# Two-layer attention and mixture of experts on one core: the block list spread over partitions, slots and products moved

## Chip, core and metric

The kernel runs on one core of one Trainium2 chip. The metric is the device time of one execution in microseconds (us), here given as the median of several runs. Engines are named as in the profile: PE (TensorE, with PEld for its weight loads), DVE (VectorE, "Vector"), ACT (ScalarE), POOL (GpSimd) and SP (SyncE, which here only issues DMAs).

## What is computed

The reference, cut to what matters: x has 32 sequences of 128 tokens of 128 features, the context 32 times 77 tokens.

```python
x = x + L0_xattn(layernorm(x), ctx, ctx)    # 16 heads of 8, softmax over 77 keys
x = x + L0_moe(layernorm(x))                # 8 experts, top 2, silu(x W1) * (x W2) @ W3, F = 256
x = x + L1_xattn(layernorm(x), ctx)         # softmax over features: q + q (k^T v) / (q sum k)
x = x + L1_moe(layernorm(x))                # 2 shared experts + 8 experts, top 2, gelu, F = 512
# top 2: topv, topi = top_k(xt @ Wg.T, 2); w = softmax(topv); out = sum over the 2 of w * expert(xt)
```

## The kernel before

Activations of all 32 tiles of 128 tokens stay in on-chip memory (`x_sb`). Work goes by 8 groups of 4 tiles (`NGRP`, `U_LAST` is group 7). Each layer is an attention part (`attention0`, `attention1`) that also routes its tokens, and a part `routed(l)` in which 40 blocks of tokens go through the experts.

Routing. For each group Vector chooses two experts per token (`choose`), PE counts them (`column_sums`, then `ranks`), GpSimd computes the exponent of the difference of the two logits (`gate_exp`), Vector makes the gates (`gates`) and the row to which each token goes (`slots`), and GpSimd scatters the rows of the group, 8 indirect DMAs, into a DRAM buffer sorted by expert (`scatter(l, group, from, to)`). After the last group's ranks PE sums the counts of all experts (semaphore `counts`, its matmul writes the same row of counts into 128 partitions). From it Vector makes the ends of the regions (`region_tails`, which lets SyncE and ScalarE write padding rows there, five and three DMAs) and the list of blocks (`block_list`, semaphore `emap`): for each of 32 slots for big blocks (256 rows) and 32 for small ones (128 rows) the expert, the first row, and a count that the load of the rows waits for. The last group's `slots` must be done before its rows are scattered; when all rows have landed GpSimd writes `mark` (semaphore `sorted`). Every Vector instruction in `block_list` waits for the one before by a semaphore (`link`).

Routed blocks. SyncE loads, in the order written in its program, the weights of 5 blocks ahead (`block_weights`) and the rows of 6 blocks ahead (`block_rows`); both read the block's numbers from the list `e_i` into registers. First blocks of the list may be spare; only rows of real ones wait for `sorted`. PE takes the blocks in order: transposes, up products, down products. Vector and ScalarE do the rest, and GpSimd scatters the results back to token order. PE enters `routed(0)` when `emap`, `bias1_ready` and `cx_v` for all groups are there. `bias1_ready` is Vector's last instruction in `attention0`, behind all of its `context_shift`s.

Context of layer 1. In layer 0's end the keys and values of the context are made for layer 1: PE does `context_keys(g)` and `context_values(g)`, Vector subtracts the maximum (`context_shift(g)`, two instructions), ScalarE copies values (`context_values`) and takes exponents (`context_exp`). `context_keys(g)` has two banks in turn and waits for the shift of group g - 2. `keep_clock(n, b)` issues n products of constants on 512 columns into bank b that nobody reads.

Order at the end of `attention0` on Vector, before: inverse sums of group 7, gates and slots of group 5, output and residual of group 7, choice of group 6, `context_shift(0)`, gates and slots of group 6, `context_shift(1)`, choice of group 7, `context_shift(2)`, tails, the list, `context_shift(3)`, gates and slots of group 7, the other shifts. In layer 1 gates and slots of group 7 stand before the list already.

Of the kernel before, what the change touches and what calls it, by code (L numbers as in the profile page):

```python
# [25 lines left out]
I32 = mybir.dt.int32  # L26
# [4 lines left out]
P = 128  # L31
# [6 lines left out]
E = 8  # L38
# [53 lines left out]
K_SPARE = K_INDEX + 2 * NSLOT  # L92
K_DONE = K_SPARE + 2 * NSLOT
# [6 lines left out]
def constants():  # L100
# [14 lines left out]
    i = np.arange(NSLOT)  # L115
    c[:, K_INDEX:K_SPARE] = np.concatenate([BLK * (i - NBIG), P * (i - NSMALL)])
    spare = E * PITCH + DSMALL * P
    c[:, K_SPARE:K_DONE] = np.repeat([spare + DBIG * BLK, spare], NSLOT)
# [102 lines left out]
def build(nc, a, out):  # L221
    ctx = ExitStack()
    with ctx:
# [59 lines left out]
        cnt = sb("cnt", [1, E])  # L283
        cnt_i = sb("cnt_i", [1, E], I32)
        til_i = sb("til_i", [1, 2, E], I32)
        til = sb("til", [1, 2, E])
        upto = sb("upto", [1, 2, E, E])
        cum = sb("cum", [1, 2, E])
        excess = sb("excess", [1, 1])
        split = sb("split", [1, E])  # L290
        edge = sb("edge", [1, 2, E + 1])
        whole = sb("whole", [1, E])
        base = sb("base", [1, 2, E])
# [5 lines left out]
        inside = sb("inside", [1, 2, NSLOT, E])  # L299
        index = sb("index", [1, 2, NSLOT])  # L300
        spare = sb("spare", [1, 2, NSLOT])
        e_i = sb("e_i", [1, 3, 2 * NSLOT], I32)
        erow = sb("erow", [1, 3, 2 * NSLOT])
# [4 lines left out]
        until = sb("until", [1, len(SETS)])  # L308
        below = sb("below", [1, len(SETS), NYB * NQ])
# [84 lines left out]
        def _(sp):  # L394
# [41 lines left out]
            def routed(l):  # L436
# [4 lines left out]
                def block_weights(u):  # L441
                    after(sp, S("y_sum"), u - NWB + 1)
                    b = column_of(u)
                    e = sp.value_load(e_i[0:1, 0, b:b + 1], min_val=0, max_val=E - 1)
                    sp.dma_start(w_blk[u % NWB][:, 0:wc], wsrc[bass.ds(e, 1)].rearrange("o p c -> p (o c)"))\
                        .then_inc(S(f"w_in{u % NWB}"), 16)

                def block_rows(u):
                    after(sp, S(f"y_out{u % NYB}"), stored(u - NXR + NYB))
                    b, n = column_of(u), tiles_of(u)  # L450
                    r = sp.value_load(e_i[0:1, 1, b:b + 1], min_val=0, max_val=E * PITCH + SPARE - n * P)
                    if u < first_real:
                        count = sp.value_load(e_i[0:1, 2, b:b + 1], min_val=1, max_val=3)
                        sp.wait_ge(S("sorted"), count)
# [53 lines left out]
        def _(pool):  # L508
# [47 lines left out]
            def attention0():  # L556
# [317 lines left out]
        def _(dve):  # L874
# [71 lines left out]
            def block_list(l):  # L946

                link(v.tensor_scalar(cnt[:], bank[4 - l][0:1, 0:E], float(P - 1), None, ALU.add))
# [4 lines left out]
                link(v.scalar_tensor_tensor(til[:, 1, :], til[:, 0, :], -2.0, til[:, 1, :], ALU.mult, ALU.add))  # L953
                link(v.tensor_tensor(upto[:], til[:].unsqueeze(2).to_broadcast([1, 2, E, E]),
                                     cst[0:1, K_LE:K_INDEX].rearrange("p (k a b) -> p k a b", k=2, a=E), ALU.mult))
# [3 lines left out]
                link(v.tensor_tensor(split[:], cum[:, 0, :], excess[:].to_broadcast([1, E]), ALU.min))  # L959
                link(v.tensor_tensor(edge[:, 0, 1:E + 1], cum[:, 0, :], split[:], ALU.subtract))  # L960
                link(v.tensor_tensor(edge[:, 1, 1:E + 1], cum[:, 1, :], split[:], ALU.add))

                def over_slots(ap):
                    return ap.unsqueeze(2).to_broadcast([1, 2, NSLOT, E])

                link(v.tensor_tensor(index[:], cst[0:1, K_INDEX:K_SPARE].rearrange("p (k i) -> p k i", k=2),
                                     edge[:, :, E:E + 1].to_broadcast([1, 2, NSLOT]), ALU.add))
# [3 lines left out]
                link(v.tensor_scalar(erow[:, 0, :], erow[:, 0, :], -1.0, 0.0, ALU.add, ALU.max))  # L971
                link(v.tensor_scalar(erow[:, 2, :].rearrange("p (k i) -> p k i", k=2), inside[:, :, :, 0], float(l + 1), 1.0,
                                     ALU.mult, ALU.add))

                link(v.tensor_tensor(whole[:], edge[:, 0, 1:E + 1], edge[:, 0, 0:E], ALU.subtract))
                link(v.tensor_tensor(base[:], cst[0:1, K_BASE:K_N].unsqueeze(1).to_broadcast([1, 2, E]), edge[:, :, 0:E],
                                     ALU.subtract))
                link(v.tensor_tensor(base[:, 1, :], base[:, 1, :], whole[:], ALU.add))
                link(v.tensor_tensor(inside[:], inside[:], over_slots(base[:]), ALU.mult))
                link(v.reduce_max(spare[:], inside[:], AX.X))  # L980
                row = erow[:, 1, :].rearrange("p (k i) -> p k i", k=2)
# [865 lines left out]
```

## Time and profile before

| | us |
|---|---|
| median of 3 runs | 782.66 (781.25 to 784.82) |
| the profiled execution | 784.91 |
| its span, first to last instruction | 782.9 |
| PE busy in it | 688.5 |
| Vector busy in it | 465.7 |
| GpSimd busy in it | 381.2 |
| ScalarE busy in it | 327.3 |

The mean granted clock of PE is 0.942 of full speed. The chain of work that ended last is 53% PE, 18% Vector, 8% issue, 5% DMA and 4% each GpSimd, ScalarE and SyncE. A busy share is a mean over the whole span; what an edit does is read where it stands. In a timeline row a bracket gives the time that the engine sat idle before, and what ended it; rows of like instructions next to each other are merged with a count.

### The profile page before, as it was taken

The numbers are of one execution on the slowest core, as the hardware profiler recorded it, in microseconds if no ns is written. First come the engines' busy times: TensorE is split into PE (matmuls) and PEld (weight loads), VectorE is DVE, ScalarE is ACT, GpSimd is POOL, SyncE is SP. The second block draws the span as 40 slices with busy tenths as digits, with TensorE's granted clock in tenths as the row PEclk, the third lists the DMA queues.
The fourth block names the chain that finished last, engine by engine and source line by source line (L and its number), as shares of the span: only waits on it lengthen the run. The fifth ranks groups of instructions, "written<-read, shape, count | busy, mean of one in ns | idle before, by whom it ended". The sixth has DMA issues, their size and how long they took to land.

```text
span 782.9 us, 15683 instructions
## 1 busy us (share of the span) xinstructions
PE 688.5 (88%) x5118; PEld 510.3 (65%) x5118; DVE 465.7 (59%) x1347; ACT 327.3 (42%) x689; POOL 381.2 (49%) x502
## 2 busy tenths in 40 slices
PE   4999999999898968889878799999999689999990
PEld 2666666566666657878766545555554389999990
DVE  2566877787677667676656667676653523324326
ACT  2344455445333232222212456667764244444440
POOL 5213176566537524555551365555555414454452
PEclk9999999999889789999997899999999979999996
DMA  6811111221101457776756000000000478877769
GB/s 164 258 12 10 10 28 26 30 30 25 32 12 35 126 166 237 215 225 204 212 165 173 0 18 21 28 29 21 24 28 27 123 234 258 270 238 246 227 196 285
DMA packets 102120, 91.34 MB, mean 117 GB/s; under 512 B 52953, under 2 KB 85849, under 8 KB 101721
## 3 DMA queue, kind: packets, MB, share of 16 engines
q1 hardware_dynamic: 86375, 68.80, 32.4%
q0 software_dynamic: 8640, 17.84, 6.4%
q10 hardware_dynamic: 7025, 3.70, 1.9%
q8 instruction: 42, 0.69, 0.4%
q14 instruction: 38, 0.30, 0.1%
HBM read 69.13 MB, written 22.72 MB: 117 GB/s over the span
## 4 chain that ended last, share of the span: by engine, by line
PE 53%; DVE 18%; issue 8%; DMA 5%; POOL 4%; ACT 4%; SPq 4%; another core or an unknown queue 3%; POOLq 0%; DVEq 0%; ACTq 0%
PE pair L1352 27%; PE pair L1640 10%; PE pair L1355 8%; DVE sm L1116 3%; DVE smax L1112 3%; POOL xs_sorted L553 2%; DMA xr<-xs_sorted 2%; PE pair L1458 2%; PE pair L1692 2%; PE pair L1473 2%; ACT xa L663 2%; DMA y_tok<-ysb,xr 1%; DMA xa<-y_tok 1%; DVE bns L1062 1%
## 5 line engine op out<-in xcount | busy, mean ns | idle before, releaser
L626 POOL DMA_INDIRECT y_tok<-ysb,xr x142 | 137.6, 969 | 145.5 <-DVE ysb L1032 116.3
L553 POOL DMA_INDIRECT xs_sorted<-xa,slot_i x128 | 130.2, 1017 | 93.5 <-DVE slot_i L939 59.0
L1352 PE MATMUL pair<-xT,w_all 128*128 128x256 f32 (+1 forms) x640 | 142.9, 369 | 0.0
L1640 PE MATMUL pair<-w_all,hT 128*128 128x128 f32 x852 | 110.8, 279 | 10.1 <-DVE hT L1019 10.0
L1352 PEld LDWEIGHTS pair<-xT,w_all 128*128 128x128 f32 x640 | 112.6, 201 | 10.4
L1640 PEld LDWEIGHTS pair<-w_all,hT 128*128 128x128 f32 x852 | 108.1, 195 | 15.1 <-issue 12.0
L801 ACT ACTIVATE hT<-pair,w_all 128x256 f32<-128x256 f32 (+1 forms) x160 | 62.0, 448 | 78.6 <-PE pair L1352 78.1
L1011 DVE COPY xT<-pair 128x256 f32<-128x256 f32 (+1 forms) x80 | 31.5, 394 | 104.9 <-PE pair L1355 88.7
L797 ACT ACTIVATE hg<-pair,w_all 128x256 f32<-128x256 f32 (+1 forms) x80 | 31.7, 447 | 93.5 <-PE pair L1352 68.3
L1112 DVE TENSOR_REDUCE smax<-pair 128x8 f32<-128x616 f32 x64 | 50.5, 788 | 33.2 <-PE pair L1352 32.8
L1352 PE MATMUL pair<-xeT_all,w_sh 128*128 128x512 f32 x128 | 69.2, 623 | 0.0
L818 ACT ACTIVATE hS<-pair,w_sh 128x512 f32<-128x512 f32 x64 | 43.9, 686 | 53.5 <-PE pair L1352 43.2
L1692 PE MATMUL pair<-hS,w_sh 128*128 128x512 f32 x128 | 65.4, 593 | 0.0
L1355 PEld LDWEIGHTS pair<-cst,sm 128*128 128x128 f32 x320 | 37.2, 151 | 26.4 <-issue 26.4
L1355 PE MATMUL pair<-cst,sm 128*128 128x128 f32 x320 | 52.8, 300 | 0.2 <-issue 0.2
L1116 DVE TENSOR_TENSOR sm<-pair,smax 128x616 f32<-128x616 f32 x64 | 51.2, 799 | 2.2
L1352 PE MATMUL pair<-hT,yS 32*128 32x308 f32 x192 | 41.8, 514 | 11.6 <-DVE sm L1116 10.0
L1355 PE MATMUL pair<-cst,xr 128*128 128x128 f32 x142 | 30.7, 288 | 18.7 <-DMA xr<-xs_sorted 7.0
L1019 DVE SCALAR_TENSOR_TENSOR hT<-pair,w_all,hg 128x256 f32<-128x256 f32 (+1 forms) x80 | 32.6, 448 | 24.2 <-remote 15.1
L701 ACT ACTIVATE wide<-pair 128x384 f32<-128x384 f32 x64 | 24.5, 434 | 44.5 <-PE pair L1355 44.5
L701 ACT ACTIVATE hS<-pair 128x384 f32<-128x384 f32 x64 | 24.6, 433 | 34.3 <-PE pair L1355 34.3
L1692 PEld LDWEIGHTS pair<-hS,w_sh 128*128 128x128 f32 x128 | 23.0, 190 | 23.7 <-issue 21.2
(194 smaller groups left out, 1100.5 us busy)
## 6 DMA issues: line engine op xcount, KB each, us to landing
w_all<-in_w SPq DMA_DIRECT2D x40, 578.0 KB
w_all<-in_w SPq DMA_DIRECT2D x40, 450.0 KB
xa<-y_tok SPq DMA_DIRECT2D x32, 256.0 KB, 5.6
xr<-xs_sorted SPq DMA_DIRECT2D x62, 130.0 KB
y_tok<-ysb,xr POOLq DMA_INDIRECT x142
xs_sorted<-xa,slot_i POOLq DMA_INDIRECT x128
out<-x_sb ACTq DMA_DIRECT2D x8, 256.0 KB, 3.1
xs_sorted<-in_pads SPq DMA_DIRECT2D x12, 130.0 KB, 4.3
```

The source lines that it names most:

```text
L553: g.indirect_dma_start(xs_dram[l], bass.IndirectOffsetOnAxis(ap=slot_i[:, i:i + 1], axis=0), xa[:, GT * c + j // TOPK, j % TOPK, :], None) ...
L626: g.indirect_dma_start(y_dram[l], bass.IndirectOffsetOnAxis(ap=xr[u % NXR][:, t, P:P + 1].bitcast(I32), axis=0), ysb[u % NYB][:, t, :], None)\
L701: s_.activation(pT[T % 2][gr][:, 0:n], bank[2 + gr % 2][:, 0:n], ACT.Exp, scale=SCALE)\
L801: s_.activation(hT[k][:, c, 0:n], src, ACT.Gelu, bias=w[:, bcol + c:bcol + c + 1])\
L818: s_.activation(hS[i % 4][:], bank[4 + i % 2][:], ACT.Gelu, bias=w_sh[:, col:col + 1])\
L1019: v.scalar_tensor_tensor(hT[k][:, c, 0:n], chunk(bank[2 * k + 1], c, BLK)[:, 0:n], w[:, bcol + c:bcol + c + 1], hg[k][:, c, 0:n], ALU.add, ...
L1112: link(v.reduce_max(smax[ab][:].rearrange("q (b h) -> q b h", b=2), score(ab), AX.X))
L1116: v.tensor_tensor(sm[ab][:, 0:SPAN].rearrange("q (b h k) -> q b h k", b=2, k=NK), score(ab), smax[ab][:].rearrange("q (b h) -> q b h", b=2 ...
L1352: return mm(out_, l_, r_, start=True, stop=True)
L1355: return nc.tensor.transpose(out_, in_, ident)
L1640: last = mm(bank[4 + k][:, t * P:(t + 1) * P], hT[k][:, c, t * P:(t + 1) * P], chunk(w, nu + c, P), start=(c == 0), stop=(c == nc_ - 1))
L1692: mm(bank[6][:], w_sh[:, wd:wd + P], hS[i % 4][:], start=(c == 0), stop=(c == NC1S - 1))\
```

## The change

`block_list` is computed with one slot per partition: partitions 0 to 31 hold the big slots, 32 to 63 the small ones. Each partition computes the counts for itself (on 64 partitions in place of one), and `inside`, which had 2 x 32 x 8 elements in one partition, has 8 in each of 64. The results `e_i` are 64 x 3 in place of 1 x 192, so the registers are loaded from another partition for each slot. The number of linked instructions goes from 26 to 27, and `low_counts`, inside `routed`, gets one more. The table of constants is 95 columns narrower. Vector's order changes: gates and slots of group 5 go in front of the inverse sums of group 7; gates and slots of group 7 go in front of the tails and the list, and `context_shift(2)` and `(3)` behind it. GpSimd's scatters of group 5 are split once more around `gate_exp` of group 6. PE gets four products of constants in three places.

```diff
@@ constants
-K_SPARE = K_INDEX + 2 * NSLOT
-K_DONE = K_SPARE + 2 * NSLOT
+K_AT = K_INDEX + NBIG
+K_SPARE = K_AT + 1
+K_DONE = K_SPARE + 1
@@ SyncE
-                    e = sp.value_load(e_i[0:1, 0, b:b + 1], min_val=0, max_val=E - 1)
+                    e = sp.value_load(e_i[b:b + 1, 0:1], min_val=0, max_val=E - 1)
...
@@ GpSimd, attention0
                 inverse_std(0, 1, "lne", U_LAST)
+                scatter(0, U_LAST - 2, 4, 6)
                 gate_exp(0, U_LAST - 1)
-                scatter(0, U_LAST - 2, 4, NPS)
+                scatter(0, U_LAST - 2, 6, NPS)
@@ Vector, block_list
-                link(v.tensor_scalar(cnt[:], bank[4 - l][0:1, 0:E], float(P - 1), None, ALU.add))
+                both, big, small = slice(0, 2 * NSLOT), slice(0, NSLOT), slice(NSLOT, 2 * NSLOT)
+                link(v.tensor_scalar(cnt[:], bank[4 - l][both, 0:E], float(P - 1), None, ALU.add))
...
-                link(v.tensor_tensor(inside[:], over_slots(edge[:, :, 0:E]),
-                                     index[:].unsqueeze(3).to_broadcast([1, 2, NSLOT, E]), ALU.is_le))
-                link(v.reduce_sum(erow[:, 0, :].rearrange("p (k i) -> p k i", k=2), inside[:], AX.X))
+                link(v.tensor_tensor(edge[big, 1:E + 1], cum[big, 0, :], split[big, :], ALU.subtract))
+                link(v.tensor_tensor(edge[small, 1:E + 1], cum[small, 1, :], split[small, :], ALU.add))
+
+                link(v.tensor_tensor(base[big, :], cst[big, K_BASE:K_N], edge[big, 0:E], ALU.subtract))
+                link(v.tensor_tensor(base[small, :], cst[small, K_BASE:K_N], edge[small, 1:E + 1], ALU.subtract))
+                link(v.scalar_tensor_tensor(base[small, :], til[small, 1, :], float(P), base[small, :], ALU.mult, ALU.add))
+
+                link(v.tensor_tensor(index[:], cst[both, K_AT:K_SPARE], edge[:, E:E + 1], ALU.add))
+                link(v.tensor_tensor(inside[:], edge[:, 0:E], index[:].to_broadcast([2 * NSLOT, E]), ALU.is_le))
+                link(v.reduce_sum(erow[:, 0:1], inside[:], AX.X))
...
+                link(v.tensor_tensor(inside[:], inside[:], base[:], ALU.mult))
+                link(v.reduce_max(begin[:], inside[:], AX.X))
...
@@ Vector, attention0
-                inverse_sums(U_LAST)
                 gates(0, U_LAST - 2)
                 slots(0, U_LAST - 2)
+                inverse_sums(U_LAST)
...
                 sums(0, U_LAST)
-                context_shift(2)
+                gates(0, U_LAST)
+                slots(0, U_LAST)
                 region_tails(0)
                 block_list(0)
-                context_shift(3)
-                gates(0, U_LAST)
-                slots(0, U_LAST)
-                for g in range(4, NGRP):
+                for g in range(2, NGRP):
                     context_shift(g)
@@ PE, attention0
                 context_values(1)
+                keep_clock(1, 4)
                 column_sums(0, U_LAST - 1)
                 ranks(0, U_LAST - 1)
+                keep_clock(2, 4)
                 kept_turned(U_LAST)
                 context_values(2)
                 logits(U_LAST)
                 context_keys(2)
                 context_values(3)
+                keep_clock(1, 4)
                 pe.wait_ge(S("slots"), U_LAST)
                 column_sums(0, U_LAST)
```

## Rows read from the trace of the kernel before

**Rows 1.** The page, its first line.
```profile
span 782.9 us, 15683 instructions
```
**Rows 2.** The chain that ended last, in order: start us, us, what.
```profile
269.12 4.01 another core or an unknown queue
...
279.28 0.46 PE pair L1355
```
**Rows 3.** Timeline of all engines, 266 to 290: start us, us, engine, line, operation.
```profile
268.42 1.08 PE L1389 MATMUL pair<-bias,ones_row 1*77 1x512 f32 x2
...
270.36 1.04 PE L1352 MATMUL pair<-wa,xeT_all 128*77 128x128 f32 x8
...
277.46 0.59 ACT L660 ACTIVATE kvm_all<-pair 77x512 f32<-77x512 f32 x1 [7.53 <-remote]
```
**Rows 4.** Timeline of GpSimd (POOL), layer 0, then layer 1.
```profile
266.06 0.96 POOL L553 DMA_INDIRECT xs_sorted<-xa,slot_i  x1 [4.56 <-DVE slot_i L939]
...
274.92 0.96 POOL L553 DMA_INDIRECT xs_sorted<-xa,slot_i  x1 [0.30 <-issue]
...
618.71 0.96 POOL L553 DMA_INDIRECT xs_sorted<-xa,slot_i  x1 [0.30 <-issue]
```
**Rows 5.** Timeline of SyncE's DMA issues (SP), layer 0, then layer 1.
```profile
256.39 8.66 SPq L462 DMA_DIRECT2D xs_sorted<-in_pads  x5
...
273.09 0.00 SPq L445 DMA_DIRECT2D w_all<-in_w  x1
...
277.44 0.33 SPq L445 DMA_DIRECT2D w_all<-in_w  x1
...
281.82 1.97 SPq L457 DMA_DIRECT2D xr<-xs_sorted  x2
...
287.90 0.33 SPq L457 DMA_DIRECT2D xr<-xs_sorted  x1
...
608.38 5.75 SPq L462 DMA_DIRECT2D xs_sorted<-in_pads  x5
...
622.76 0.34 SPq L445 DMA_DIRECT2D w_all<-in_w  x1
...
625.52 0.33 SPq L445 DMA_DIRECT2D w_all<-in_w  x1
```
**Rows 6.** Timeline of Vector (DVE), layer 1, last instruction of the list.
```profile
616.47 0.25 DVE L986 CAST e_i<-erow 1x192 int32<-1x192 f32 x1
```
**Rows 7.** Timeline of Vector, layer 0, the list of blocks.
```profile
255.21 0.15 DVE L948 TENSOR_SCALAR cnt<-pair 1x8 f32<-1x8 f32 x1
...
257.97 0.75 DVE L968 TENSOR_TENSOR inside<-edge,index 1x512 f32<-1x512 f32 x1
258.76 0.67 DVE L970 TENSOR_REDUCE erow<-inside 1x64 f32<-1x512 f32 x1
...
262.75 0.25 DVE L986 CAST e_i<-erow 1x192 int32<-1x192 f32 x1
```
**Rows 8.** Timeline of all engines: Vector at the inverse sums.
```profile
232.47 0.96 DVE L1125 RECIPROCAL rden<-pair 128x128 f32<-128x128 f32 x1 [1.50 <-PE pair L1473]
```
**Rows 9.** Timeline of Vector, first instruction of the last group's gates.
```profile
264.24 0.16 DVE L921 TENSOR_SCALAR wsum<-exd 128x4 f32<-128x4 f32 x1
```
**Rows 10.** Stretches: length, busy time by engine, granted clock, DMA share, GB/s.
```profile
245.00:250.00 5.00, 4.70 (x22) 4.03 (x22) 3.27 (x14) 1.95 (x4) 3.78 (x5) 0.66 0.15 45
...
260.00:265.00 5.00, 5.00 (x17) 3.41 (x18) 4.59 (x15) 1.37 (x3) 1.20 (x2) 0.50 0.30 74
...
275.00:280.00 5.00, 0.45 (x1) 0.18 (x1) 1.81 (x4) 2.52 (x5) 0.96 (x2) 0.59 0.47 143
```
**Rows 11.** Timeline of PE in layer 0 around the choices.
```profile
243.25 0.19 PE L1352 MATMUL pair<-ones_b,oh 128*64 128x1 bf16 x1 [0.60 <-DVE high L906]
...
245.30 1.11 PE L1355 MATMUL pair<-cst,xa 128*128 128x128 f32 x4 [0.97 <-ACT xa L663]
```
**Rows 12.** The chain that ended last, in layer 1.
```profile
603.81 0.86 PE pair L1692 x2
```

More of the change, by code:

```diff
@@ L282, in build @@
         csum = sb("csum", [P, NCH, P], BF16)
[L283 to L293, printed above, removed]
+        cnt = sb("cnt", [2 * NSLOT, E])
+        cnt_i = sb("cnt_i", [2 * NSLOT, E], I32)
+        til_i = sb("til_i", [2 * NSLOT, 2, E], I32)
+        til = sb("til", [2 * NSLOT, 2, E])
+        units = sb("units", [2 * NSLOT, 2, E])
+        upto = sb("upto", [2 * NSLOT, 2, E, E])
+        cum = sb("cum", [2 * NSLOT, 2, E])
+        excess = sb("excess", [2 * NSLOT, 1])
+        split = sb("split", [2 * NSLOT, E])
+        edge = sb("edge", [2 * NSLOT, E + 1])
+        base = sb("base", [2 * NSLOT, E])
         tail_i = sb("tail_i", [1, E], I32)
@@ L298, in build @@
         slot_i = sb("slot_i", [P, NPAIR], I32)
[L299 to L303, printed above, removed]
+        inside = sb("inside", [2 * NSLOT, E])
+        index = sb("index", [2 * NSLOT, 1])
+        begin = sb("begin", [2 * NSLOT, 1])
+        e_i = sb("e_i", [2 * NSLOT, 3], I32)
+        erow = sb("erow", [2 * NSLOT, 3])
         mark = sb("mark", [1, 1])
@@ L308, in build @@
         until = sb("until", [1, len(SETS)])
+        last = sb("last", [1, 1])
         below = sb("below", [1, len(SETS), NYB * NQ])
@@ L978, in block_list @@
[L978 to L981, printed above, removed]
-                link(v.scalar_tensor_tensor(row, index[:], 0.0, cst[0:1, K_SPARE:K_DONE].rearrange("p (k i) -> p k i", k=2),
-                                            ALU.is_lt, ALU.mult))
@@ new lines, in block_list @@
+                link(v.tensor_scalar(erow[:, 0:1], erow[:, 0:1], -1.0, 0.0, ALU.add, ALU.max))
+                link(v.tensor_scalar(erow[:, 2:3], inside[:, 0:1], float(l + 1), 1.0, ALU.mult, ALU.add))
+                link(v.tensor_tensor(inside[:], inside[:], base[:], ALU.mult))
+                link(v.reduce_max(begin[:], inside[:], AX.X))
+                link(v.tensor_tensor(begin[:], begin[:], index[:], ALU.add))
+                link(v.scalar_tensor_tensor(erow[:, 1:2], index[:], 0.0, cst[both, K_SPARE:K_DONE], ALU.is_lt, ALU.mult))
@@ L986, in block_list @@
+                link(v.tensor_tensor(erow[:, 1:2], erow[:, 1:2], begin[:], ALU.add))
                 v.tensor_copy(e_i[:], erow[:]).then_inc(S("emap"), 1)
@@ L990, in low_counts @@
                 n = len(SETS)
-                link(v.tensor_tensor(until[:], pre[:], edge[:, 0, E - 1:E].to_broadcast([1, n]), ALU.add))
-                link(v.tensor_tensor(below[:, :, NSTILL:NB], index[:, 0, ISTILL:NBIG].unsqueeze(1)
+                link(v.tensor_tensor(last[:], edge[0:1, E - 1:E], edge[0:1, E:E + 1], ALU.subtract))
+                link(v.tensor_tensor(until[:], pre[:], last[:].to_broadcast([1, n]), ALU.add))
+                link(v.tensor_tensor(below[:, :, NSTILL:NB], cst[0:1, K_INDEX + ISTILL:K_AT].unsqueeze(1)
                                      .to_broadcast([1, n, NB - NSTILL]),
```

34 lines of the change are left out of this document (11 added, 23 removed).

## Prediction

> **What bounds it now.** I read the page for the span, 782.9 us [rows 1], then the chain that ended last through the two places where the list of blocks is made, then each engine's timeline there. The reader is to see three things. First, in layer 0 the routed blocks start on PE at 279.28, behind the bias addition on Vector, and the chain in front of it holds 4.01 us put down to "another core or an unknown queue" [rows 2]. PE began its last values product of the context at 270.36, yet ScalarE copied those values at 277.46, after 7.53 us of idling [rows 3]: PE's signals arrived late. Second, this lateness coincides with GpSimd's scatters issued back to back. The last group's eight run from 266.06 to 275.88, and the lateness ends 1.6 us after; ahead of them stands a pause of 4.56 [rows 4]. SyncE is slow in the same stretch: its weight loads at 273.09 and 277.44 stand 4.35 apart, where 2.75 is normal without scatters (622.76 to 625.52) [rows 5]. Third, in layer 1 nothing but SyncE's order of loads stands before the blocks: the list is written at 616.72, the second weights leave at 622.76 [rows 5, 6], and PE follows the rows loaded between them.
>
> **The list of blocks.** Before, 26 linked Vector instructions from 255.21 to 263.00, 7.8 us [rows 7]; in layer 1 the same ones end at 616.72 [rows 6]. After, 27. Those on 8 elements stand 0.19 apart. Four work on 512 elements in one partition, 0.75 and 0.67, and then the same pair again [rows 7]; they become 8 elements in 64 partitions. I price them as 0.15 and a gap of 0.04: 4 x 0.19 = 0.76 in place of 3.0, so 2.25 less. Seven on 64 or 192 elements (0.25 for the last [rows 7]) shrink by 0.3 together. One instruction more costs 0.19. Sum: 2.35 less, 5.4 us. No row shows few elements in exactly 64 partitions; the row with 128 partitions and 4 elements (0.16 [rows 9]) and those with 512 bound the list between 5.4 and, were none of the four to shrink, 7.9. I take 5.4, by the nearest row. The Trainium skill, "VectorE: DVE Perf Modes", section on SBUF-source operations' fixed extra latency, gives the time as a constant plus the elements of the free dimension; by its 58 cycles at 0.96 GHz an instruction on 8 elements would take some 0.07, an estimate that the rows' 0.16 replaces.
>
> **Layer 1.** Its order is untouched, so the list ends at 616.72 - 2.35 = 614.4. SyncE ends its five tail loads at 614.13 (608.38 plus 5.75 [rows 5]) and waits for the list, so the loads of block 0 leave 2.2 us earlier. From 616.72 to the second weights at 622.76 SyncE took 6.0 where a normal pair and the way to the first load need 3.5: it is slow until about 1.5 us past GpSimd's last scatter (618.71 plus 0.96 [rows 4]). That end does not move; the loads in front of it do. Bounds: the slow stretch takes half of the gain back, -1.0, or a pair slips wholly in front of it, -2.6. I take -2.3. All later row loads follow in SyncE's order and PE follows them; behind it PE is the chain, so nothing absorbs it.
>
> **Layer 0, what is ready when.** Gates and slots of the last group begin at 264.24 [rows 9] and release GpSimd for 266.06 [rows 4]; without their way to it they take 1.55. They now stand in front of the list, from about 254.2. The tails, just before 255.21, move to about 256.2, the list ends at about 261.7 instead of 263.0. SyncE's tail loads start 0.9 later, and SyncE was busy with them until 265.05 (256.39 plus 8.66 for five [rows 5]), past the old end of the list; so the earlier list alone brings nothing. GpSimd's last eight scatters come without the pause: they end at 261.8 + 8 x 1.265 = 271.9 instead of 275.88. The mark that rows are sorted goes from about 277.5 to 273.5, but the first load that needs it left at 281.82 [rows 5]: nothing by itself.
>
> **What this collides with.** Fourteen scatters now run without a pause from about 254.3, so SyncE is slow through its tail loads (9.6 us instead of 8.66) and its first loads: weights at 267.5 and 271.8, then 2.75 a pair, rows of block 6 at 286.8 against 287.90 [rows 5]. These need block 0's result as well, some 8.6 us behind PE's start (279.28 to 287.90). So PE's start decides, unless SyncE keeps 4.3 a pair for longer. Bounds of this cap: 284 and 290.5.
>
> **Context keys behind the list.** Shifts 2 to 7 all come after it now. A keys product waits for the shift two before it, so products 4 to 7 start only at about 263.1; before, PE ran them beside the list. At full clock one costs 1.94 (268.42 to 270.36) and a values product 1.0 [rows 3]. After 263.1: four keys and three values, 10.8, a last shift 1.4, bias 0.3: blocks start at 275.6, a gain of 3.7. But PE now idles from about 258 to 263.1. In this trace the idle stretch before 279.28 took the granted clock to 0.59 in its window [rows 10], which is the 1.2 GHz level for most of it; at that level, 0.50 in 260 to 265 [rows 10], each of these products takes nearly twice as long. Some 6 to 10 us at half clock cost 3 to 5: start at 279 to 280.9. I take 279.6, +0.3. The Trainium skill, "TensorE: Matmul & The Clock Gate", section "What's actually happening", says that throttled is the default state and activity releases it. By that rule the shifts behind the list work against the change, and the trace agrees in sign.
>
> **Products in waits.** A product on 512 columns is two records, 0.86 us [rows 12]. One stands in a wait of 0.60 before 243.25, two in 0.97 before 245.30 [rows 11], the last ahead of the last group's column sums, in a wait that I take as short as the first. They overrun by 0.26, 0.75 and about 0.3. Against that, the stretch from 245 to 250 ran at 0.66 [rows 10]: with the transposes at 245.30, whose four took 1.11 [rows 11], about 1.3 comes back if the clock stays up (a third of 5 us is lost, less what waits hide). Net 0.1 late at the last group's choice; bounds -1.0 and +1.4.
>
> **Slots of the third last group in front of the inverse sums.** They fill Vector's idle 1.50 before 232.47 [rows 8] and take 1.8: inverse sums start 0.3 later. GpSimd's split of the scatters frees the norm 0.7 earlier; ScalarE has two copies of PE's values ahead of its use, so this is hidden. Cost +0.2, bounds -0.4 and +0.4. One more small instruction per layer in the counts of low rows lies in Vector's idle time beside the blocks; map entries read from other partitions are as many register loads on SyncE as before; the smaller table of constants comes in behind other inputs: nothing for each, 0.2 a load at worst for the second, hidden but for the first pairs.
>
> **Sum.** Layer 1 -2.3; start of layer 0's blocks +0.3, which has the products' 0.1 and the inverse sums' 0.2 in it, as they precede the list: -2.0. The profiled execution lasted 784.91, 2.0 more than its span, and gives 782.9; the median of the runs shown, 782.66, is 2.25 lower and gives 780.6.
>
> **Rivals.** (a) The lateness ends with the scatters, and PE keeps the full clock or regains it at once: layer 0's blocks start at 275.6, so -3.7 - 2.3, 776.7. For it: the scatters end 4 us earlier, and the late signals held 277.46. Against: PE's idling before 263.1 and SyncE's cap. Chance 0.27. (b) The other side: PE's signals are held through the run of fourteen, up to the 6.0 us of the values product at 270.36. Keys 4 reach Vector at 272.8, the shift ends at 274.2, and two keys and one values product at half clock, 9.7, a shift and the bias remain: 285.6, +6.3; with layer 1, 786.7. It decides from a start at 285.5 on. For it: the run is nearly twice as long. Against: in the run of eight Vector got the keys before the last inside it. Chance 0.1. (c) The shorter list has no effect, because the slow stretch of SyncE takes all of layer 1's gain: 782.9. Chance 0.13. My forecast, 780.6 with its own range of 778.8 to 783.5, has 0.5.
>
> **Numbers.** 0.5% is 3.9 us, about what a measurement of this kernel can tell from no change: below 778.7 is faster, above 786.6 slower. Faster takes (a) nearly whole and a little of the forecast: 0.29. Slower takes half of (b) and as much for the bounds above: 0.09. Same: 0.62. The range, 776.2 to 785.0, leaves out the tails of (a) and most of (b).
>
> **What would show it.** The list at 5.4 us in both layers; layer 1's first weights 2.2 us sooner after the tails; fourteen scatters with gaps of 0.3 alone; PE idle for 4 to 5 us before keys 4 and a granted clock near 0.5 behind it; blocks starting right behind Vector's bias. It is wrong if the list does not shrink, if the clock stays at 1.00 through the keys, or if SyncE's tails take over 12 us.

## The result, and the profile after

The changed kernel took 788.75 us (median of 7 runs, 786.04 to 790.52), the kernel before on the same chip 781.91 (7 runs, 779.52 to 785.9). The medians differ by 6.8 us. The ratio is given as 1.0081, 95% interval 1.0052 to 1.0109, which is slower by 6.3 us. The forecast was 780.6, range 776.2 to 785.0, so the time lies outside it. What came in layer 0 is rival (b), to which the forecast gave 0.1, and in layer 1 rival (c). The profiled execution of the changed kernel took 789.36 us.

The profile after is read in the order of the forecast: the span, the list, then layer 0 engine by engine, then layer 1. The page's first line:

```profile
span 787.2 us, 15704 instructions
```

The list of blocks in the changed kernel, timeline of Vector in layer 0, first two instructions, the compare and the reduction that worked on 512 elements before, and the last:

```profile
254.17 0.15 DVE L953 TENSOR_SCALAR cnt<-pair 64x8 f32<-64x8 f32 x1
254.35 0.37 DVE L954 CAST cnt_i<-cnt 64x8 int32<-64x8 f32 x1
...
257.89 0.16 DVE L974 TENSOR_TENSOR inside<-edge,index 64x8 f32<-64x8 f32 x1
258.08 0.15 DVE L975 TENSOR_REDUCE erow<-inside 64x1 f32<-64x8 f32 x1
...
259.57 0.20 DVE L983 CAST e_i<-erow 64x3 int32<-64x3 f32 x1
```

From 254.17 to 259.77 are 5.6 us, against 7.8 before [rows 7]. The two wide instructions went from 0.75 and 0.67 to 0.16 and 0.15. The list did what it was priced at.

The chain that ended last, in the changed kernel, behind the list:

```profile
262.57 0.04 issue
262.63 10.39 another core or an unknown queue
273.04 0.70 DVE cxm L1075
...
283.94 1.75 issue
285.69 0.46 PE pair L1351
```

In front of layer 0's blocks stood 4.01 us of an unnamed release before [rows 2]; now it is 10.39. The blocks start at 285.69 instead of 279.28, 6.4 later, as much as the kernel lost. The other engines say what it is made of. Timeline of GpSimd, first and last of fourteen scatters, all 0.30 apart:

```profile
252.45 1.03 POOL L556 DMA_INDIRECT xs_sorted<-xa,slot_i  x1 [0.20 <-issue]
...
268.96 0.96 POOL L556 DMA_INDIRECT xs_sorted<-xa,slot_i  x1 [0.30 <-issue]
```

Timeline of SyncE's issues in the same kernel, layer 0, then layer 1:

```profile
255.28 18.31 SPq L465 DMA_DIRECT2D xs_sorted<-in_pads  x5
274.43 0.38 SPq L448 DMA_DIRECT2D w_all<-in_w  x1
...
613.56 5.98 SPq L465 DMA_DIRECT2D xs_sorted<-in_pads  x5
623.37 0.77 SPq L448 DMA_DIRECT2D w_all<-in_w  x1
626.83 0.36 SPq L460 DMA_DIRECT2D xr<-xs_sorted  x1
627.97 0.34 SPq L448 DMA_DIRECT2D w_all<-in_w  x1
```

The five padding copies took 18.31 us to issue, where they took 8.66 before [rows 5]. SyncE came out of them 3.7 us after the last scatter's end at 269.92. Taken one by one they left at 255.28, 257.33, 262.36, 269.46 and 273.06: the gaps grow to 7.1 as the run goes on. In layer 1 the first four left 1.3 apart (613.56 to 617.49) although GpSimd's last eight scatters had begun at 614.59, so the loads are not slow beside every scatter.

Timelines of PE and then of Vector (the same kernel): the keys of shifts 4, 6 and 7 on PE, and the waits of Vector for them:

```profile
261.11 1.99 PE L1385 MATMUL pair<-bias,ones_row 1*77 1x512 f32 x2 [4.02 <-issue]
263.03 1.99 PE L1389 MATMUL pair<-wa,xeT_all 128*77 128x128 f32 x8
...
274.50 1.98 PE L1385 MATMUL pair<-bias,ones_row 1*77 1x512 f32 x2 [4.53 <-DVE hS L1076]
...
281.96 1.99 PE L1389 MATMUL pair<-wa,xeT_all 128*77 128x128 f32 x8
```
```profile
273.04 0.69 DVE L1075 TENSOR_REDUCE cxm<-pair 77x64 f32<-77x512 f32 x1 [10.47 <-remote]
...
278.44 0.69 DVE L1075 TENSOR_REDUCE cxm<-pair 77x64 f32<-77x512 f32 x1 [2.48 <-PE pair L1389]
...
283.98 0.69 DVE L1075 TENSOR_REDUCE cxm<-pair 77x64 f32<-77x512 f32 x1 [4.13 <-PE pair L1389]
```

PE had the keys of shift 4 done at 265.0, but Vector started on them only at 273.04, 3.1 us after the last scatter's end. ScalarE waited in the same way for the next values, which PE had done at 266.7 (its timeline):

```profile
273.14 0.59 ACT L664 ACTIVATE kvm_all<-pair 77x512 f32<-77x512 f32 x1 [11.42 <-remote]
```

This is called holding below. Whether PE's signal left late or the waiting engines took it late isn't told apart by these rows. Once the holding was over PE ran keys 6, values 7 and keys 7 from 274.50 to 283.95, at 1.98 and 1.99 for what takes 1.08 at full clock [rows 3]. The stretches of the changed kernel show the two clock levels (granted clock is the third number from the end):

```profile
245.00:250.00 5.00, 5.00 (x37) 3.97 (x36) 4.45 (x19) 1.71 (x3) 3.70 (x4) 1.00 0.15 45
...
270.00:275.00 5.00, 0.49 (x1) 0.33 (x2) 1.82 (x3) 1.86 (x4) 0.00 (x0) 0.92 0.08 27
275.00:280.00 5.00, 5.00 (x18) 3.32 (x16) 2.30 (x4) 0.25 (x1) 0.09 (x1) 0.50 0.66 195
280.00:285.00 5.00, 3.94 (x11) 1.94 (x10) 0.98 (x2) 1.63 (x3) 0.00 (x0) 0.50 0.58 159
```

In 245 to 250 the constants' products kept 1.00 where before had 0.66 [rows 10]. After the idle stretch up to 274.50 PE had the lower level, 0.50, for the products that decide.

In layer 1 the gain did not come. From the start of the tail loads to the second weights are 14.41 us (613.56 to 627.97), and were 14.38 (608.38 to 622.76, [rows 5]). The list was no longer what SyncE waited for: Vector wrote it by 619.9, GpSimd's last scatter ended at 624.53, and SyncE's first load of rows left 2.3 us after that. Vector's and GpSimd's timelines:

```profile
619.71 0.16 DVE L983 CAST e_i<-erow 64x3 int32<-64x3 f32 x1
```
```profile
623.57 0.96 POOL L556 DMA_INDIRECT xs_sorted<-xa,slot_i  x1 [0.30 <-issue]
```

Only the first weights left sooner, by 0.8 (9.81 after the start of the tail loads for 10.58); the first rows (13.27 for 13.25) and the second weights did not. Ten further traces of kernels with the new list on chips of this kind have 14.70 to 14.78 to the second weights, so the missing gain is no accident of one trace; before has one trace on this kind.

So the profile gives +6.4 at layer 0's blocks and nothing at layer 1's first loads. The tail loads of layer 1 stand 5.2 later than before and the span is 4.3 longer; no edit is behind what came back in between. Two traces of the changed kernel on chips of one kind differ by 8.6 us in span (787.2 and 795.8), so one trace's span isn't split finer than that here. The start of the tail loads moves too, from 252.82 to 258.26 in five traces of kernels that are alike up to there. The time from the tail loads to the blocks is steadier: 30.41 and 30.48 in two traces of the changed kernel, 22.89 in the one of before, so 7.5 longer.

### The profile page after: what moved, and what is told of

It reads as the page before. It is cut to its first block, busy times and chain, and to the rows that moved or that the text cites. A ratio compares the mean times of both kernels' runs of the same rounds, so it can differ in the third digit from the quotient of the medians.

```text
span 787.2 us, 15704 instructions
## 1 busy us (share of the span) xinstructions
PE 689.2 (88%) x5126; PEld 507.5 (64%) x5126; DVE 460.7 (59%) x1351; ACT 326.9 (42%) x689; POOL 381.9 (49%) x502
## 4 chain that ended last, share of the span: by engine, by line
PE 49%; DVE 20%; issue 10%; POOL 5%; SPq 5%; ACT 4%; DMA 3%; another core or an unknown queue 3%; POOLq 0%; DVEq 0%; ACTq 0%
PE pair L1348 26%; PE pair L1639 9%; PE pair L1351 7%; DVE sm L1114 3%; POOL xs_sorted L556 3%; DVE smax L1110 3%; PE pair L1454 2%; PE pair L1691 2%; ACT xa L667 2%; PE pair L1469 1%; DMA xr<-xs_sorted 1%; DVE bns L1060 1%; POOL rstd L536 1%; SPq L454 1%
## 5 line engine op out<-in xcount | busy, mean ns | idle before, releaser
L1348 PE MATMUL pair<-xT,w_all 128*128 128x256 f32 (+1 forms) x640 | 141.1, 365 | 0.0
L1348 PEld LDWEIGHTS pair<-xT,w_all 128*128 128x128 f32 x640 | 110.7, 198 | 10.0
L1639 PE MATMUL pair<-w_all,hT 128*128 128x128 f32 x852 | 109.0, 276 | 5.7 <-DVE hT L1017 4.3
```

The costliest lines, as they stand in the source:

```text
L1348: return mm(out_, l_, r_, start=True, stop=True)
L1639: last = mm(bank[4 + k][:, t * P:(t + 1) * P], hT[k][:, c, t * P:(t + 1) * P], chunk(w, nu + c, P), start=(c == 0), stop=(c == nc_ - 1))
```

## Experiments

Eighteen runs of twelve kernels were made, on five chips. The chips are of two kinds. On three (here the first kind) the kernel before takes 782 to 789 us, as in the first comparison; on two (the second kind) 752. All times of an experiment are compared with before on its own chip. Two theories of the loss stand behind them. T1 (A1 in the first expectations): the run of fourteen scatters holds PE's signals and SyncE's loads. T2 (A2 there): shifts 2 to 7 stand behind the list, so PE idles and then runs the keys late and at half clock. In the first expectation A is that the moves in layer 0 did the harm and not the list, B that the list or its registers cost something.

**What part of the change costs it.** The first four ran on one chip of the second kind, where before took 752.02. The new list alone, all orders and PE's program as before:

```
-                gates(0, U_LAST)
-                slots(0, U_LAST)
+                context_shift(2)
                 region_tails(0)
                 block_list(0)
-                for g in range(2, NGRP):
+                context_shift(3)
+                gates(0, U_LAST)
+                slots(0, U_LAST)
+                for g in range(4, NGRP):
                     context_shift(g)
...
-                keep_clock(1, 4)
```

> The kernel before with the new list of blocks and its narrower constants alone; every order as before. Theory A (the moves in layer 0 did the harm, the list itself helps): SyncE's five tail loads again near 9 us, blocks of layer 0 start where they did, within 1 us, layer 1's rows 2 us earlier, so 2.0 to 2.5 us below the kernel before. Rival B (the list on 64 partitions, or its registers read from many partitions, costs something in the blocks): no gain or a loss of 1 to 4 us, spread over both routed parts.

Measured: 748.27, ratio 0.9944 (0.9921 to 0.9967). The new list by itself gains 3.7 us there, more than the 2.0 to 2.5 expected. Its blocks do not start where they did: they start 15.65 us after the tail loads (245.11 to 260.76), against 20.87 for before on the other chip of this kind (245.86 to 266.73).

The last group's gates and slots behind the list again, shifts 2 to 7 behind them:

```
-                gates(0, U_LAST)
-                slots(0, U_LAST)
                 region_tails(0)
                 block_list(0)
+                gates(0, U_LAST)
+                slots(0, U_LAST)
```

> The changed kernel with the last group's gates and slots behind the list again, so that GpSimd pauses in front of its last eight scatters; shifts 2 to 7 stay behind the list. Theory A1 (fourteen scatters without a pause hold SyncE and PE's signals): tail loads back from 18.3 to about 9 us, Vector's 10.5 us wait for PE gone, blocks of layer 0 start at 280 to 281.5 on the old time axis, so 3 to 5 us below the changed kernel. Rival A2 (the harm is the shifts behind the list, which leave PE idle and at half clock): the start stays within 1.5 us of the changed kernel's 285.7.

Measured: 753.68, ratio 1.0017 (0.9990 to 1.0044). On this chip the edit did not part the run. GpSimd had only just reached the last group's scatters when their slots were written (its timeline, first of the last eight):

```profile
253.26 0.96 POOL L556 DMA_INDIRECT xs_sorted<-xa,slot_i  x1 [0.30 <-DVE slot_i L943]
```

One shift back in front:

```
+                context_shift(2)
                 gates(0, U_LAST)
                 slots(0, U_LAST)
                 region_tails(0)
                 block_list(0)
-                for g in range(2, NGRP):
+                for g in range(3, NGRP):
```

> The changed kernel with context_shift(2) in front of the gates and slots of the last group; shifts 3 to 7 stay behind the list, the run of fourteen scatters stays. Theory A1: tail loads stay near 18 us and the gain is small, 0 to 2 us below the changed kernel, as keys 4 are made during the list but their signal is held. Rival A2: PE is busy beside the list, keeps the clock, and 4 to 5 us come back.

Measured: 748.85, ratio 0.9973 (0.9946 to 1.0000). The changed kernel without the constants' products (`keep_clock` lines taken out):

> The changed kernel without the four products of constants. If they hold the clock up and cost nothing, taking them away makes it 0.5 to 1.5 us slower; if they only overrun their waits, 0.5 to 1 us faster. Both theories of the harm expect the start of layer 0's blocks to stay within 1.5 us, as the products lie before the list.

Measured: 751.91, ratio 1.0001 (0.9977 to 1.0026), which can't be told from 1.0027 for the changed kernel with them, on the next chip. On this chip the price lies with the place of the shifts: with one of them in front, the run of fourteen scatters costs nothing that shows; with none in front, the kernel doesn't gain. What I did not expect is that five tail loads took 5.9 to 6.2 us in all four, and every wait of Vector of over 1.4 us between the list and the blocks ended with PE's products and not unnamed, so nothing was held, and this chip could not test what the first trace showed.

**The same chip for before and after.** The next batch ran on another chip of the second kind (before 751.75).

> The kernel before, unchanged, for a trace of it on the chip of the other experiments. On that chip the tail loads of the experiments took 5.9 to 6.2 us for five, not 8.66, and no signal of PE came late. Theory T2 (what costs layer 0 is that shifts 2 to 7 stand behind the list, so that PE idles and then runs the keys at half clock): before shows here too five tail loads in about 5.9 us, keys at 1.9 for two records or less, and bias behind the written list by some 11 to 13 us. Theory T1 (what costs it is the run of scatters that holds the signals and SyncE's loads): before shows tail loads of 8 us or more and late signals, as its first trace did.

> The changed kernel, unchanged. T2: about 1.002 of before on the experiments' chip (752 to 755 us), bias behind the list by some 19 to 21 us, with waits of Vector for keys of 2.5 and 4.1 in between, and no held signal; the first chip's 1.0081 has then a part that comes from held signals there. T1: 1.008 again, with tail loads of 18 us for five and PE's signals 10 us late.

Before was profiled once more, at 750.46; the changed kernel took 753.69, ratio 1.0027 (1.0005 to 1.0048). PE's timelines of the two, before first (from keys 4 on), then the changed kernel (from values 4 on):

```profile
248.54 1.47 PE L1389 MATMUL pair<-bias,ones_row 1*77 1x512 f32 x2
...
253.85 1.08 PE L1389 MATMUL pair<-bias,ones_row 1*77 1x512 f32 x2 [1.94 <-DVE wide L1078]
...
266.73 0.45 PE L1355 MATMUL pair<-cst,xr 128*128 128x128 f32 x1 [1.74 <-issue]
```
```profile
246.15 1.04 PE L1348 MATMUL pair<-wa,xeT_all 128*77 128x128 f32 x8
252.77 1.98 PE L1385 MATMUL pair<-bias,ones_row 1*77 1x512 f32 x2 [5.58 <-DVE wide L1076]
...
258.31 1.98 PE L1385 MATMUL pair<-bias,ones_row 1*77 1x512 f32 x2
...
270.74 0.30 PE L1351 MATMUL pair<-cst,xr 128*128 128x128 f32 x1 [1.75 <-issue]
```

The row at 248.54 is keys 4 of before: they ran beside the list. In the changed kernel they stand behind it at 252.77, after 5.58 us of idling, and they and keys 5 run at half clock. Blocks start 4.0 later, without any holding. The tail loads show that (SyncE's issues, changed kernel, this chip):

```profile
246.96 5.88 SPq L465 DMA_DIRECT2D xs_sorted<-in_pads  x5
...
582.56 5.74 SPq L465 DMA_DIRECT2D xs_sorted<-in_pads  x5
589.71 0.38 SPq L448 DMA_DIRECT2D w_all<-in_w  x1
```

Here layer 1 does gain: first weights 7.15 us after the start of the tails, against 9.06 for before on this chip (576.52 to 585.58), 1.9 of the 2.3 forecast; to the second weights it is 1.8 (10.12 against 11.90).

GpSimd waits for the padding copies ahead of the last group's scatters (one line):

```
+                pool.wait_ge(S("xs_padded"), 16 * E)
                 scatter(0, U_LAST, 0, NPS)
```

> The changed kernel, but GpSimd waits until the copies of padding rows have landed before it issues the last group's scatters. T1, with contention between those copies and the scatters: 4 to 6 us faster than the changed kernel, layer 0's bias at most 14 us behind the list. T2: no gain, within 1 us of the changed kernel, since the shifts stay where they are.

Measured: 754.04, ratio 1.0026 (1.0001 to 1.0050), the same as the changed kernel, as T2 wants on this chip. Here the run was parted, by 3.33 us. And the changed kernel with Vector's end of the attention part in the order of before (shift 2, tails, list, shift 3, gates and slots of the last group, other shifts):

> The changed kernel with Vector's end of the attention part in the order of before (shift 2, tails, list, shift 3, then gates and slots of the last group, then the other shifts); it keeps the new list, the constants' products, the early slots of the third last group and the split of the scatters. T2: as fast as the new list alone, 0.994 to 0.995 of before, 4 to 6 us faster than the changed kernel, bias some 11 us behind the list. T1: the same if the run of fourteen scatters is what costs, so this one tells apart only whether products and early slots matter: theory P says that they are worth nothing (0.994), theory P- that they cost 1 us or more (0.996 or above).

Measured: 749.98, ratio 0.9968 (0.9945 to 0.9991), 3.7 us less than the changed kernel.

**The clock, and the small parts.** This batch fell on a chip of the first kind (before 788.57). Six more constants' products in PE's idle stretch:

```
                 for g in range(3, NGRP):
+                    if g == 4:
+                        keep_clock(6, 7)
                     context_keys(g)
```

> The changed kernel with six more constants' products (512 columns each, two records, some 0.86 us each at full clock) on PE ahead of the keys of shift 4, in PE's idle stretch of 5.58 us behind the values before them. T2 in its form 'half clock' (the idle stretch lowers the granted clock, and the keys behind it run at half of it, 3.9 instead of 2.0 each): the keys run at 2.0 to 2.2, bias comes 14 to 16 us behind the list instead of 19.1, and the kernel takes 3 to 5 us less than the changed kernel, ratio to before 0.996 to 0.999. T2 in its form 'lateness alone' (the serial way keys, shift, keys is what costs, whatever the clock): at most 1.5 us less, ratio 1.001 to 1.003.

Measured: 791.71, ratio 1.0042 (1.0015 to 1.0070). Its timelines of PE and of Vector:

```profile
259.95 5.31 PE L1348 MATMUL pair<-cst 128*128 128x512 f32 x12
265.19 1.08 PE L1385 MATMUL pair<-bias,ones_row 1*77 1x512 f32 x2
...
268.10 1.08 PE L1385 MATMUL pair<-bias,ones_row 1*77 1x512 f32 x2
...
273.30 0.27 PE L1389 MATMUL pair<-wa,xeT_all 128*77 128x128 f32 x1 [2.64 <-issue]
275.41 0.37 PE L1389 MATMUL pair<-wa,xeT_all 128*77 128x128 f32 x1 [1.83 <-issue]
```
```profile
276.31 0.69 DVE L1075 TENSOR_REDUCE cxm<-pair 77x64 f32<-77x512 f32 x1 [10.21 <-remote]
```

The filling did its work: keys 4 and 5 ran at full clock. It did not help their way to Vector. Keys 4 ended at 267.3 and Vector waited until 276.31. The run of fourteen ended at 272.9, five tail loads took 18.49 us, and even PE's own stream stood still inside keys 5 for 2.64 and 1.83. This is the holding with no half clock in front of it. The ratio is below the 1.008 of the changed kernel, but on another chip and with intervals that overlap, so whether the clock gave a part isn't told; from tail loads to blocks the trace has 29.39, 1.0 less than the changed kernel.

On the same chip, the list alone once more, then the list with the early slots of the third last group and the split of scatters, then the list with the products:

> The new list alone, a second time, to stand beside the next two on one chip: 0.994 to 0.996 of before.

> The new list, and the slots of the third last group in front of the inverse sums with the split of GpSimd's scatters; no constants' products, Vector's end of the attention part as before. My forecast put +0.2 us on this part (bounds -0.4 and +0.4): within 1 us of the new list alone. If this part is what made the version with the old order of the tail slower than the list alone (0.9968 against 0.9944 on two chips), it is 1 to 2 us slower than the list alone.

> The new list and the four constants' products, without the early slots of the third last group. My forecast put +0.1 us on them (bounds -1.0 and +1.4): within 1 us of the list alone, with the granted clock of the stretch near the last transposes held at 1.00. If the products are what made the version with the old order of the tail slower, this one is 1 to 2 us slower than the list alone.

Measured: 787.97, ratio 0.9982 (0.9955 to 1.0008); 788.57, 0.9993 (0.9970 to 1.0017); 786.92, 0.9982 (0.9952 to 1.0011). Neither small part can be told from nothing. The list alone, too, is worth less than on the second kind, where it had 0.9944.

**Parting the run where signals are held.** Another chip of the first kind, before 788.16.

> The changed kernel, unchanged. Chips of two kinds have shown so far: on one kind (before at 788.6 us in the run with the extra products, 781.9 in the first comparison) the tail loads take 18 us beside the run of fourteen scatters and PE's signals come 10 us late; on the other (752) they take 6 and none comes late. T1: on a chip of the first kind 1.006 to 1.010 of before; on one of the second kind 1.001 to 1.004.

Measured: 794.94, ratio 1.0079 (1.0051 to 1.0107): the first comparison over again, with five tail loads in 18.42 us.

> The changed kernel with gates and slots of the last group behind the list again, shifts 2 to 7 behind them: it parts the run of fourteen scatters into six and eight, with a pause of some 4 us, and leaves the shifts as late as they are. On a chip of the first kind T1 (the run holds the signals) gives tail loads of 8 to 9 us instead of 18, no wait of Vector of 10 us, and 3 to 5 us less than the changed kernel; T2 (late shifts and half clock alone) gives the changed kernel's time within 1 us. On a chip of the second kind both give within 1 us of it.

Measured: 792.10, ratio 1.0046 (1.0013 to 1.0079). Here the run was parted, by 2.24 us. The tail loads took 9.82 and no wait of 10 us is left. PE, however, idles 6.01 and then runs at half clock:

```profile
266.23 1.98 PE L1385 MATMUL pair<-bias,ones_row 1*77 1x512 f32 x2 [6.01 <-DVE wide L1076]
```

In this trace gates and slots of the last group took 3.8 us on Vector (261.07 to 264.85), with pauses of 0.25 to 0.97 between its instructions, against 1.6 without a pause in the changed kernel (252.36 to 253.99). So Vector's own stream stands still too, and part of what this edit leaves of the loss lies there.

> The changed kernel, with GpSimd waiting for the copies of padding rows before the last group's eight scatters. On a chip of the first kind T1 gives tail loads of 8 to 9 us, a pause of 2 to 4 us between six scatters and eight, and 2 to 5 us less than the changed kernel. T2, and any chip of the second kind: no gain.

Measured: 789.92, ratio 1.0027 (0.9997 to 1.0057), 5.0 us less than the changed kernel on the same chip. GpSimd's, SyncE's and Vector's timelines:

```profile
256.38 0.96 POOL L556 DMA_INDIRECT xs_sorted<-xa,slot_i  x1 [0.30 <-issue]
264.22 0.95 POOL L556 DMA_INDIRECT xs_sorted<-xa,slot_i  x1 [6.88 <-DMA xs_sorted<-in_pads]
...
273.05 0.96 POOL L556 DMA_INDIRECT xs_sorted<-xa,slot_i  x1 [0.30 <-issue]
```
```profile
252.82 9.44 SPq L465 DMA_DIRECT2D xs_sorted<-in_pads  x5
```
```profile
275.77 0.69 DVE L1076 TENSOR_REDUCE cxm<-pair 77x64 f32<-77x512 f32 x1 [6.88 <-remote]
```

With a pause of 6.88 the tail loads take half the time. The last two keys, done by PE at 270.3 and 273.3, are then held beside the second run of eight, and Vector starts on them 1.8 us after its end.

> The changed kernel with Vector's end of the attention part in the order of before. On a chip of the first kind both theories give some 0.998 of before, as the list alone and the list with the products had there (0.9982 both), so 6 to 8 us less than the changed kernel; on one of the second kind 0.994 to 0.998.

Measured: 786.41, ratio 0.9983 (0.9952 to 1.0013), 8.5 us less than the changed kernel. In its trace too the last keys reach Vector (276.26, after 5.85) only 2.0 us after the last scatter's end at 274.24.

**Both cures, and one shift in front.** A third chip of the first kind, before 782.08. The wait for the padding copies together with the six products:

> The changed kernel with both cures: GpSimd waits for the padding copies before the last group's scatters, and six constants' products fill PE's idle stretch ahead of the keys of shift 4. If holding and half clock are the two causes of the loss and add up, it stands where the list alone stands: 0.996 to 0.999 of before on a chip of the first kind (where the wait alone gave 1.0027), 0.996 to 0.999 on one of the second (where the wait alone gave 1.0026). If the half clock costs nothing and the late shifts are what is left, it stands where the wait alone does, 1.002 to 1.003.

Measured: 785.39, ratio 1.0045 (1.0018 to 1.0072). The two cures do not add up in the time. PE's keys run at full clock and end at 274.0, but the wait puts the last scatter's end at 276.1, and Vector has the keys at 277.78, 1.7 after it; the blocks start at 279.48, 23.21 after the tail loads. And shift 2 in front of gates and slots, the run of fourteen kept:

> The changed kernel with shift 2 back in front of gates, slots, tails and list; the run of fourteen scatters stays. On a chip of the second kind 0.997 to 0.999, as before (0.9973). On one of the first kind the run still holds signals and tail loads (18 us for five), so 1.002 to 1.006, slower than the old order of the tail (0.9983) though as many shifts stand ahead but one.

Measured: 787.98, ratio 1.0065 (1.0033 to 1.0097). The same kernel had 0.9973 (0.9946 to 1.0000) on a chip of the second kind. Its timelines of SyncE, PE and Vector show the run's price, and PE's also that the next keys (6) wait for Vector to shift those that came late:

```profile
256.24 16.68 SPq L465 DMA_DIRECT2D xs_sorted<-in_pads  x5
```
```profile
271.60 1.98 PE L1386 MATMUL pair<-bias,ones_row 1*77 1x512 f32 x2 [7.12 <-issue]
```
```profile
270.14 0.69 DVE L1075 TENSOR_REDUCE cxm<-pair 77x64 f32<-77x512 f32 x1 [8.69 <-remote]
```

The ratios side by side (before is 1; first kind, then second kind):

| kernel | first kind | second kind |
|---|---|---|
| changed kernel | 1.0081, 1.0079 | 1.0027 |
| changed, slots behind the list | 1.0046 | 1.0017 |
| changed, wait for padding copies | 1.0027 | 1.0026 |
| changed, one shift in front | 1.0065 | 0.9973 |
| changed, old order of Vector's tail | 0.9983 | 0.9968 |
| list alone | 0.9982 | 0.9944 |

## Why the prediction was wrong, point by point

**The list of blocks.** Right: 5.6 us for 5.4 forecast. The one instruction that stands out above its price is the second, a cast of 0.37.

**Layer 0, the step that failed.** Under "Context keys behind the list" the forecast let PE's keys 4 reach Vector as soon as they were done, priced only the half clock, and took 279.6. They were held: done at 265.0, they were taken up at 273.04, 8.0 later and 3.1 us after the fourteenth scatter's end. Rival (b) had put keys 4 at Vector at 272.8 and the blocks' start at 285.6; the trace has 273.04 and 285.69. The mechanism was seen and its chance was wrong. That its times agree to 0.3 us is in part luck: its 272.8 less its 6.0 of holding has keys 4 done at 266.8, and they were done 1.8 earlier and held 2.0 longer. I weighed against it that "in the run of eight Vector got the keys before the last inside it". A run of fourteen isn't a run of eight made longer: three traces with the run (two kernels) had tail loads of 18.3 to 18.5 us, and 16.7 with one shift in front; eight kernels without it on like chips had 8.1 to 9.8. The forecast of 9.6 for these tail loads is the same error seen on SyncE; it named 12 us as the point that would prove it wrong.

**How much is which.** On the first kind, going back to the old tail order takes 8.5 us off. Parting the run while the shifts stay late takes 2.8 or 5.0, with a pause of 2.2 or 6.9. So the run costs a third to over half of that. The 5.0 are shown (1.0079 to 1.0027, ten runs each on one chip, 790.72 to 797.93 against 786.28 to 794.47, though the intervals of the two ratios just overlap; the same wait changed nothing on the second kind, 1.0027 to 1.0026); the 2.8 alone would lie within the intervals, and rest on the tail loads beside them. The rest goes with the late shifts, and on the second kind, where nothing is held, they are the whole loss: 3.7 us between the changed kernel and the old order. One shift in front brought 1.0017 down to 0.9973 there; on the first kind, with the run kept, the same shift left 1.0065. Whether what costs there is their lateness or the half clock is argued from rows only (two keys and two values products took 11.1 us from 252.77 to 263.85, and at full clock one of each takes 2.9, keys at 265.61 to keys at 268.52 in the old order on the first kind, so 5.8); the filling that was to tell them apart fell on a chip of the first kind, where it showed the holding instead. Why both cures together left 1.0045 stays open: that trace's blocks start 23.21 after its tail loads, 0.3 later than before and 3.0 sooner than with the wait alone (26.18, ratio 1.0027), so either before usually starts earlier than its one trace shows, or something behind the blocks' start costs. The start of the blocks is not passed on whole in any case: on the second kind it came 5.0 earlier with the old order than in the changed kernel (18.76 against 23.78 from the tail loads), and the time fell by 3.7. In the traces with an early start the first blocks wait for their rows (1.36 and 1.77 in the list alone).

**Layer 1.** Also wrong, on this kind of chip: -2.3 forecast, 0.0 in the trace. Rival (c) came here, the stall of SyncE until after the last scatter took the whole gain; the forecast's bound of half, -1.0, was too kind. On the second kind 1.9 came. That is one part of why the list alone has 0.9944 there and 0.9982 here; the other is in layer 0, where its blocks start 5.2 sooner after the tail loads than before's there (15.65 for 20.87) and 1.3 sooner here (21.60 for 22.89).

**The sum.** With (b)'s +6.3 and no gain in layer 1, the median of 782.66 gives 789.0; measured 788.75. By the 781.91 of before in the same comparison it would be 788.2. Since two terms of (b) were 2 us off against each other, so close a fit is not to be leaned on.

**Products in waits, and the slots of the third last group.** Priced +0.1 and +0.2. The list with the one or the other lies within 1.1 us of the list alone on one chip, so these prices fit, with intervals of some 2 us. The clock they were to keep was kept, 1.00 for 0.66, and no effect of it could be measured.

**What the forecast named as signs.** List at 5.6: right. Layer 1's first weights 2.2 sooner: wrong, 0.8. Fourteen scatters 0.3 apart: right. PE idle 4 to 5 us before keys 4, 4.02, and 0.50 to 0.55 behind: right. Blocks right behind Vector's bias: right. Tail loads over 12 us, which was to prove the forecast wrong: 18.31. The Trainium skill, "TensorE: Matmul & The Clock Gate", section "What's actually happening", has throttled as the default state that activity releases. The trace agrees in sign: after 4.53 us of idling the two records took 1.98 instead of 1.08.

**A version that beats both.** The new list alone, with the orders and PE's program of before: 0.9944 (0.9921 to 0.9967) on the second kind, 0.9982 (0.9955 to 1.0008) on the first. It beats the changed kernel on both, and before for certain on the second only.

## What to carry to other kernels

Closing a gap in one engine's run of DMA issues may take away the only window in which other engines get on. Where a trace shows one such release late after a run of eight, price a longer run by its end and not by the delay seen so far, and give that case the greater chance. Before something is moved in front of a dependent chain of another engine, count which parts of that chain ran beside it; four late keys cost here more than an earlier mark could bring, as no load waited for the mark.

## What the runs showed of the hardware

One kernel runs at 752 us on some chips and at 782 to 789 on others of the same type, with a granted clock of 0.965 and 0.942 in the profiled runs. One thing that sets them apart in the traces is what happens late in a row of indirect scatters issued by GpSimd back to back. On the first kind SyncE's loads (up to 7.1 us from one tail load to the next, against 1.3 undisturbed), PE's instruction stream (2.64 and 1.83 us in the middle of one product), Vector's (3.8 us for gates and slots instead of 1.6) and the waits of Vector and ScalarE for PE stand still for microseconds, mostly until 1.6 to 3.9 us after the last scatter's end (once 0.2 us before it). On the second, five tail loads take 5.74 to 6.23 us whatever GpSimd does. What is shared between these engines was not found, and that the scatters are the cause of the 30 us between the kinds is not shown: in the two traces of before 17 of them lie between PE's first and last transposes of layer 0's blocks (119.2 against 101.9 us), and what makes them was not looked for. An edit's sign can hang on this: the version with one shift in front is 1.0065 on the one and 0.9973 on the other.
